# VectorE's side work in the order of the gathers, and the first step's tanh between two chunks of a one-hot, in a four-layer graph kernel

## What is computed

```python
# x: (8, 1024, 128) float32, adj: (8, 1024, 1024) of 0 and 1, about 16 ones in a row
def layer_0(A, X, W, b):                       # sampled neighbours
    scores = where(A != 0, -arange(N), -inf)
    vals, idx = top_k(scores, 25)              # the first 25 neighbours of each node
    feats = where(valid, X[idx], -inf)
    agg = feats.max(axis=2)                    # (and 0, where a node has 25 or fewer)
    return relu(concat([X, agg]) @ W + b)

def layer_1_and_2(h, adj, W, a):               # graph attention
    z = h @ W
    e = leaky_relu((z @ a1)[:, None] + (z @ a2)[None, :], 0.2)
    return elu(softmax(where(adj > 0, e, -9e15)) @ z)

def layer_3(x, adj, att_W, W0, b0, W1, b1):    # attention once, then two steps
    att = softmax((x @ att_W) @ x.T / sqrt(128) + where(adj == 1, 0, -1000))
    for W, b in ((W0, b0), (W1, b1)):
        x = tanh(att @ (x @ W + b))
    return x

for layer in (layer_0, layer_1, layer_2, layer_3):
    x = layer_norm(x + layer(x))
```

## Time and profile before

| what | us |
|---|---|
| median of 3 executions | 1954.62 |
| lowest and highest | 1948.86 and 1959.94 |
| the profiled execution's own time | 1953.58 |
| its span, first to last instruction | 1951.8 |
| PE busy in it | 1666.7 (85%) |
| POOL busy in it | 1471.4 (75%) |
| DVE busy in it | 1413.3 (72%) |
| ACT busy in it | 1126.7 (58%) |

### The profile page before, as it was taken

How to read it: one execution, slowest core, us unless ns; L and a number is a source line. 1 busy time by engine, 2 the same in 40 slices (tenths; PEclk the granted TensorE clock), 3 DMA queues, 4 the chain that set the end, 5 groups by cost and what they waited for, 6 DMA issues and landing times.

```text
span 1951.8 us, 29181 instructions
## 1 busy us (share of the span) xinstructions
PE 1666.7 (85%) x9655; PEld 1308.6 (67%) x9700; DVE 1413.3 (72%) x3406; ACT 1126.7 (58%) x1517; POOL 1471.4 (75%) x2191
## 2 busy tenths in 40 slices
PE   4777898979889899899989899997988899896877
PEld 2655675757758577677748677675767687584746
DVE  5874888668876788668885788758886688745631
ACT  5665756646665765657566565558556565652252
POOL 6888888888888887888788887888888887880000
PEclk9989899989999899998999899998999899997889
DMA  7231433343342333334233432434333422311020
GB/s 194 71 83 45 106 75 110 87 107 76 77 131 75 101 78 94 109 91 118 76 115 75 113 78 75 126 77 112 83 101 86 131 55 64 107 43 38 1 65 11
DMA packets 154177, 168.88 MB, mean 87 GB/s; under 512 B 103133, under 2 KB 120426, under 8 KB 154026
## 3 DMA queue, kind: packets, MB, share of 16 engines
q1 hardware_dynamic: 119594, 96.43, 18.2%
q0 software_dynamic: 34432, 70.59, 14.1%
HBM read 142.29 MB, written 4.19 MB: 75 GB/s over the span
## 4 chain that ended last, share of the span: by engine, by line
POOL 32%; PE 31%; DVE 17%; issue 9%; ACT 5%; DVEq 4%; DMA 2%; POOLq 0%; ACTq 0%; SPq 0%
POOL gathered L565 24%; POOL pause L570 8%; PE big L1013 7%; PE spare L905 6%; PE big L937 4%; DVE pooled L1331 3%; DVEq L73 2%; DVE probs_t L1458 2%; PE big L1004 2%; PE big L1154 1%; PE big L1089 1%; DVE keys L1228 1%; ACT hot L634 1%; PE big L1111 1%; PE big L995 1%
## 5 line engine op out<-in xcount | busy, mean ns | idle before, releaser
L565 POOL DMA_INDIRECT gathered<-in_x_dram,rows x1076 | 1107.1, 1029 | 246.9 <-issue 163.3
L905 PE MATMUL spare<-hot,x_part 128*128 128x512 f32 x1440 | 366.7, 407 | 28.5 <-DVE hot L1379 18.9
L570 POOL MEMSET pause<- 32x256 bf16 x1076 | 357.6, 332 | 42.0
L905 PEld LDWEIGHTS spare<-hot,x_part 128*128 128x128 f32 x1440 | 271.3, 194 | 94.7 <-issue 19.4
L634 ACT ACTIVATE hot<-running,minus_count 128x2048 fp32r<-128x2048 bf16 (+1 forms) x131 | 250.8, 1914 | 85.1 <-PE spare L905 65.0
L637 ACT ACTIVATE hot<-hot,plus_one 128x2048 fp32r<-128x2048 f32 (+1 forms) x131 | 251.4, 1919 | 4.3
L1331 DVE TENSOR_REDUCE pooled<-gathered 128x128 f32<-128x2176 f32 (+2 forms) x56 | 218.2, 3897 | 32.0 <-DMA gathered<-in_x_dram,rows 30.5
L1013 PEld LDWEIGHTS big<-values,probs_t 128*128 128x128 f32 x1792 | 224.7, 203 | 8.5
L1013 PE MATMUL big<-values,probs_t 128*128 128x129 f32 x1792 | 227.7, 288 | 0.4
L1379 DVE TENSOR_SCALAR hot<-running 128x2048 fp32r<-128x2048 bf16 (+1 forms) x131 | 167.6, 1302 | 26.5 <-PE big L905 11.7
L1458 DVE SCALAR_TENSOR_TENSOR probs_t<-side,col_gain,adj_t 128x1024 f32<-128x1024 f32 x128 | 154.6, 1276 | 27.2 <-ACT side L693 27.2
(11 more groups left out here) (203 smaller groups left out, 2613.8 us busy)
## 6 DMA issues: line engine op xcount, KB each, us to landing
adj_in<-in_adj_dram SPq DMA_DIRECT2D x128, 512.0 KB
gathered<-in_x_dram,rows POOLq DMA_INDIRECT x1076, 2.5
xs<-in_x_dram SPq DMA_DIRECT2D x8, 512.0 KB, 4.7
out_dram<-xs SPq DMA_DIRECT2D x8, 512.0 KB, 3.2
adj_t<-adj_bf SPq DMA_TRANSPOSE x64
packed_t<-group_bits SPq DMA_TRANSPOSE x28, 2.7
w_sb<-in_L_gnn_W_dram SPq DMA_DIRECT2D x1, 128.0 KB
w_sb<-in_L_gnn_W_dram SPq DMA_DIRECT2D x2, 64.0 KB
```

The costliest lines, as they stand in the source:

```text
L565: (late_gathered if late else rows_gathered[t % RING]).raised_by(pool.indirect_dma_start(out=gathered[:, t % RING, k * C:(k + 1) * C], out ...
L570: last = nc.gpsimd.memset(pause[quarter:quarter + 32, k // (4 * PAUSED), :], 0.0)
L905: last = nc.tensor.matmul(pick_bank(b, q), x_parts[part][:, m, :], hot[:, place_of(b, q, m), :], start=(m == 0 and part == 0), stop=(m == ...
```

## The change

Three things are changed. In the table `SIDE` poolings and list pieces have other places. On ACT, `make_hot` takes the chunks as an argument; the two chunks of hot 11 stand apart, the first ahead of the first four tanh of the first step and the second ahead of the last four. On PE, pick 11 stands whole between the turns of the two halves of the first step's result. On DVE the pooling at "attention" goes ahead of maxima 7 and 8 and hot 9, and the place "half" is gone.

```diff
--- before.py
+++ after.py
@@ -109,16 +109,14 @@
         "gat 1": [("members", 1, 1)],
         "gat 1 heads": [("keys", 1, 2), ("pool", 1, 0)],
         "gat 2": [("members", 1, 2)],
-        "gat 2 heads": [("keys", 1, 3), ("pool", 1, 1)],
+        "gat 2 heads": [("pool", 1, 1), ("keys", 1, 3)],
         "attention": [("pool", 1, 2)],
-        "tile 1": [("pool a", 1, 3)],
-        "tile 2": [("pool b", 1, 3)],
-        "tile 3": [("members a", 1, 3)],
-        "tile 4": [("members b", 1, 3)],
-        "tile 5": [("members c", 1, 3)],
-        "steps": [("pool", 1, 4), ("keys", 2, 0), ("members", 2, 0)],
-        "last step": [("pool", 1, 5)],
-        "half": [("pool", 1, 6)],
+        "tile 0": [("members a", 1, 3)],
+        "tile 1": [("members b", 1, 3)],
+        "tile 2": [("members c", 1, 3), ("pool a", 1, 3)],
+        "tile 3": [("pool b", 1, 3)],
+        "steps": [("pool", 1, 4), ("keys", 2, 0), ("members", 2, 0), ("pool", 1, 5)],
+        "last step": [("pool", 1, 6)],
         "end": [("pool", 1, 7)]}
 
 
@@ -614,13 +612,13 @@
                 bank = side[:, 0:512] if two_banks and j % 2 == 1 else spare[:, :]
                 count_taken.raised_by(nc.scalar.copy(running[:, j, :], bank))
 
-            def make_hot(b, q):
+            def make_hot(b, q, chunks=range(CHUNKS)):
 
                 h, s = half_and_slot(b, q)
 
                 s += gathered_slots(b, h * HALF) - GATHERED_FIRST
                 first = isinstance(b, int) and b == 0
-                for c in range(CHUNKS):
+                for c in chunks:
                     if (first and c == 0) or (not first and MADE_BY[q][c] != "A"):
                         continue
                     chunk = hot_chunk(b, q, c)
@@ -752,11 +750,11 @@
                     if t >= 2:
                         act.wait_ge(att_turned.sem, att_turned.at(b, t - 1))
                         att_t_ready.raised_by(nc.scalar.copy(probs_t[:, :, (t - 2) * P:(t - 1) * P], side_t))
-                if exists(b, 1, B, in_loop):
-                    make_hot(b + 1, 11)
                 act.wait_ge(recip_ready.sem, recip_ready.at(b, 1))
                 for t in range(T):
                     if t % HALF == 0:
+                        if exists(b, 1, B, in_loop):
+                            make_hot(b + 1, 11, [t // HALF])
                         act.wait_ge(att_heads.sem, att_heads.at(b, t // HALF + 1))
                     last = nc.scalar.activation(first_rows[:, t, :], low_t[:, t, :], ACT.Tanh, scale=recip[:, t:t + 1])
                     if t % HALF == HALF - 1:
@@ -1136,10 +1134,8 @@
                 turn_first(0)
                 if exists(b, 1, B, in_loop):
                     spare_maxed(b + 1, 10)
-                    pick_tiles(b + 1, 11, range(T // CHUNKS))
+                    pick(b + 1, 11)
                 turn_first(1)
-                if exists(b, 1, B, in_loop):
-                    pick_tiles(b + 1, 11, range(T // CHUNKS, T))
                 add_bias(high_t, 3)
                 for h in range(2):
                     pe.wait_ge(first_ready.sem, first_ready.at(b, h + 1))
@@ -1524,11 +1520,11 @@
                 gat(b, slot, 1, in_loop)
                 gat(b, slot, 2, in_loop)
                 picks = exists(b, 1, B, in_loop)
+                side_work(b, slot, "attention", in_loop)
                 if picks:
                     max_pick(b + 1, 7)
                     max_pick(b + 1, 8)
                     make_hot(b + 1, 9)
-                side_work(b, slot, "attention", in_loop)
                 for t in range(T + 1):
                     if t < T:
                         dve.wait_ge(logits_psum.sem, logits_psum.at(b, t + 1))
@@ -1557,7 +1553,6 @@
                         head[:, HALF * h:HALF * h + HALF, :].rearrange("p t c -> p (t c)"), ALU.add))
                     half_stats(slot, h)
                     if h == 0:
-                        side_work(b, slot, "half", in_loop)
                         if picks:
                             make_hot(b + 1, 14)
                             max_pick(b + 1, 13)
```

## The result

The changed kernel takes 1939.76 us (median of four executions, 1937.78 to 1940.68) against 1954.49 us (four, 1948.86 to 1959.94): the ratio is 0.9925, with the interval 0.9902 to 0.9948. It is faster by 14.7 us. The forecast was 1937 in a range from 1929 to 1947, so it was right in its direction and off by 3 us in its size. Part of that nearness is luck: the claim that both halves of the change count did not hold, and the time for which POOL is held was put too low. What follows says how the forecast came out near all the same.

What follows compares the result with a forecast made beforehand. POOL's gathers and the PE, ACT and DVE loop bound the kernel together. With 17.75 us relief and 3.1 us per graph, the later loop puts the last tile 7 pooling 17.6 us earlier: 1937 us, range 1929 to 1947.

Steps and rivals of the forecast that it cites:

- both halves of the change count: Claim that speeding up POOL alone meets the PE, ACT and DVE loop at once, under 1 us spare in three graphs.
- The two loops: POOL's gathers, and "main" (PE, ACT and DVE through four layers), meeting at tile 7's pooling; neither alone gives the time.
- the six gaps: POOL's waits before tile 4's gather for tile 1's pooling, 2.97 to 6.21 us; 21.95 us above the ordinary 0.83 each.
- Part 1: Tile 1 pooled ahead of pair 3's keys, ending 6.28 us earlier; POOL's net relief 17.75 us, bounds 21.95 and 14.6.
- one cost appears: Hot 7 on DVE now meets a gather and can hold POOL: 0 to 1.22 us per graph, taken as 0.7.
- Parts 2, 3 and 5: DVE moves of poolings of tiles 2, 3, 6 and pair 3's list: taken as 0; list bounds 1.6 loss, 1 gain.
- Part 4: Between attention steps, hot 11 and tanh interleaved, pick 11 whole: main gains 3.1 us per graph, bounds 1.6 and 3.1.
- isn't later: At the last gathered graph, POOL's late rows (1762.25 - 17.75 + 1.4) don't come after tile 7's pooling start, 1744.6 us.
- (a): Rival: main gains nothing, as later DVE maxima or late hot 12 eat the gain; 1944.6 us, chance 0.13.
- (b): Rival: POOL gains nothing, another wait replaces its gaps; only the last stretch shortens by 3.1 us; 1951.5 us, chance 0.08.
- (c): Rival: hot 7 doesn't hold POOL, relief 21.95 us; 1933.5 us, or 1931.5 with list gain; inside the forecast's spread.
- (d): Rival: shifted DVE hots hold POOL's gathers 7 us more per graph over five graphs; 1968.5 us, chance 0.03.

Runs made afterwards that it cites:

- e3: Kernel before with one line changed: pooling of tile 1 ahead of the keys of pair 3; 1937.32 us, ratio 0.9927.
- e4: Changed kernel with the keys of pair 3 again ahead of the pooling of tile 1, all other edits kept; 1951.92 us, ratio 1.0011.
- e2: Kernel before with only the ACT and PE edits (four tanh between the chunks of hot 11, pick 11 whole); 1948.52 us, ratio 0.9981.
- e1: Changed kernel with ACT and PE between the attention steps as before, all DVE moves kept; 1945.37 us, ratio 0.9967.

## Why the prediction was right

**What bounds the kernel.** The two loops and the six gaps were read rightly, and the sum of the gaps (21.95 us) was the stock from which the gain came: POOL's waits for poolings went from 27.8 us in 7 gaps to 1.7 in 2. That "both halves of the change count" was wrong. The swap alone gave all of it (e3), all else 0.7 us (e4). That the measured gain came within 3 us of the forecast doesn't bear this claim out.

**Part 1, the relief.** The step was right, its price too small. POOL's waits are 22.0 us less in all, as forecast, but the last gather came 13.6 us earlier instead of 17.75: POOL was held 8.3 us longer, where 6 x 0.7 = 4.2 us had been put down. At hot 7 the price was right: 0.68 in the row, 3.9 us over all graphs. The step that failed is "one cost appears", at hot 7 alone: hot 10 holds POOL 1.8 us longer than before, hot 8 0.9, and instructions on `xs` 2 to 3 us, against 1.9 us less at the keys. In e3, which moves nothing else, the 3.9 us at hot 7 are there as well and are made up for at the keys, so its busy time is 1471.9 us against 1471.4. The 7.8 us more of the changed kernel come with the other moves. Without the swap these had a busy time of 1471.3 us (e4), 2.7 above e2 without them.

**Parts 2, 3 and 5.** On main they were neutral, as forecast. From the first row maximum to the last it is 30.7 to 30.8 us before and 30.6 to 30.7 in the changed kernel, and from hot 12 to the pooling of tile 7, less the idle time, 26.2 us in both. The pooling of tile 6 was waited for in the first graph (6.4 us) and in the last gathered one (2.96 us), the second of which the prediction had named as a sign of being wrong; what it cost isn't known. On POOL "cost nothing" failed: the runs with and without these moves are 8 and 3.4 us apart on the first chip (e3 and e1, e2 and e4). The traces show more held time on POOL with them; whether that is all of it isn't shown.

**Part 4, between the steps.** The timelines of PE and of DVE in the changed kernel, graph 3:

```profile
1046.21 0.60 PE L1095 MATMUL side<-ident,work 128*128 128x128 f32 x4
1046.57 2.09 PE L903 MATMUL spare<-hot,x_part 128*128 128x512 f32 x8
1049.23 2.12 PE L903 MATMUL spare<-hot,x_part 128*128 128x512 f32 x8 [0.57 <-ACT hot L635]
...
1054.05 3.89 PE L903 MATMUL spare<-hot,x_part 128*128 128x512 f32 x16
```
```profile
1047.46 4.06 DVE L1327 TENSOR_REDUCE pooled<-gathered 128x128 f32<-128x2176 f32 x1
...
1052.04 0.69 DVE L1387 TENSOR_TENSOR best_t<-best_t,spare 128x512 f32<-128x512 f32 x1
```

PE no longer idles 2.85 us before the first turn, waits 0.57 us for chunk 1 (0.5 forecast), picks 2.09 us a half instead of 3.50 at the low clock, and starts pick 12 7.8 us after the last product (8.3 forecast, 11.5 before). DVE no longer idles before maximum 11. All steps as put down.

What the place gained can be read from the first row maximum of layer 3 to maximum 11, before and then changed, graph 3:

```profile
1002.52 1.22 DVE L1535 TENSOR_REDUCE neg_max<-big 128x1 f32<-128x1024 f32 x1 [2.41 <-PE big L1115]
```
```profile
998.08 1.22 DVE L1531 TENSOR_REDUCE neg_max<-big 128x1 f32<-128x1024 f32 x1 [2.59 <-PE big L1113]
```

Maximum 11 starts at 1060.12 and at 1052.04, so 57.6 us became 54.0. Before, it was 57.6 us in five graphs and 56.0 in two; now it is 53.2 to 54.2. In the mean that is 3.3 us less, against 3.1 forecast.

What it is worth to main's whole period is blurred by the clock. The windows from one pooling of tile 7 to the next give the granted clock of each graph; of the kernel before the third, of e3 the fifth, of the changed kernel the second (the columns are those of the earlier trace rows, the clock is the third number from the end):

```profile
862.00:1088.00 226.00, 201.83 (x1183) 159.01 (x1188) 174.85 (x428) 137.84 (x186) 187.41 (x281) 0.95 0.36 95
```
```profile
1300.00:1522.00 222.00, 198.01 (x1178) 156.09 (x1179) 173.95 (x428) 137.34 (x186) 188.79 (x282) 0.95 0.37 96
```
```profile
636.00:859.00 223.00, 198.50 (x1176) 157.94 (x1181) 174.76 (x428) 137.04 (x185) 189.79 (x281) 0.95 0.35 96
```

Main's period without the idle time before tile 7 was 224.8 us in this one of the kernel before, 222.05 in that of e3, 219.9 in that of the changed kernel. In e3, whose ACT and PE are those of before, graphs at 0.98 take 219.1 and 219.3 us, and graphs at 0.95 take 221.9, 222.05 and 221.7. At 0.95 the changed kernel takes 218.3, 219.9, 219.1 and 218.3: 3.0 us less in the mean. This agrees with the 3.3 us above, but it is the weaker reading: the mean clock of a graph doesn't fix its period (the kernel before takes 224.8 us at 0.95 where e3 takes 222). By both, part 4 was sized rightly.

**Where main went, then.** The forecast took main's period of before as given (it had 1 graph in 6 at 0.97, the others from 0.93 to 0.95) and made main the bound only where its period asked for it. In e3 two graphs of six stood at 0.98, and main's own period was 220.9 us in the mean where it had been 223.0. So the swap alone could give 15.3 us and not 10. The trace shows where: from the pooling of tile 7 to the next hot it took 26.3 to 26.5 us in four graphs of the kernel before, three of them at a granted clock of 0.80 or 0.81, and 24.0 to 24.5 us in all of e3, where the clock behind the first graph was 0.86 or 0.93. Whether the shorter standstills bring the higher clock or chance does can't be told from one trace of each.

**The end.** Forecast: the split pooling of tile 7 starts at 1744.6 and its late part isn't held by POOL. It started at 1743.50, but the late part waited 3.05 us for the gather and came at 1749.54, where 1744.6 + 3.07 (the distance before, with no wait) = 1747.7. The step "isn't later" failed, by the held time above. (The 1.4 us in it have no row behind them. The changed kernel's rows give 2.64 us from the start of the last gather to the late part; with that the forecast had POOL's rows ready at 1745.4.) These 1.9 us, and a tail behind the late part that was 1.3 us longer, make the 3.1 between 1936.0 forecast and 1939.07. The forecast was near because of its form, a maximum of two loops: POOL's last gather was 4.2 us later than thought, but main had been put down as 2.3 us later than POOL there, so that only the rest of POOL's error reached the end. That was luck, not a sized term: had main been put down as late as POOL, the whole 4.2 us would have shown.

**The rivals.** (a), main gains nothing, and (b), POOL gains nothing, didn't occur in the changed kernel. (c), a full relief of 21.95, is nearly e3's 20.2. (d), more holding of POOL by hots, is real but was 0.7 us a graph above the sized value, not 7. One execution of e1 had 15 us more in all (1486.7 us), and was the longest of its six.

## What to carry to other kernels

Where an in-order engine releases buffers to the engine that sets the time, look at what stands right ahead of the release: 6.3 us of keys ahead of one pooling cost up to 5.4 us a graph, and exchanging two entries was worth as much as a change of three engines. Measure the parts of a change one by one: here one part carried the gain, and another cost 3 to 8 us that a third paid back. When work on VectorE is moved, compare GpSimd's busy time before and after, not only its waits: it grew by 8.3 us here with the same instructions. And don't count one trace's period as a constant of a loop: its clock differs from graph to graph.

## What the runs showed that was not expected

- POOL's busy time was between 1468.6 and 1486.7 us over six orders of the same instructions. Part of it goes with the edit (hot 7 with the swap, hot 10 with DVE's other moves), and part may differ from one execution to another.
- A memset of 0.30 us on POOL is held beside a hot like a gather, and most of the change's added held time stands in the pauses.
- Half the pause gave 1894.1 us in one kernel on one chip and 2434.06 and 2441.68 us in two others on another, in which all engines but POOL stood idle for issue. What makes the difference is open.
- The kernel before took 1952.58 us on one chip and 1967.81 us on another, and the changed kernel's gain was 15 and 21 us.
